# Causal mask of the transposed scores: a GpSimd select on the probabilities in place of one matrix product per diagonal block

## What is computed

```python
qkv = (h @ qkv_w + qkv_b).reshape(B, T, 3, H, HD)
q, k, v = [qkv[:, :, i].transpose(0, 2, 1, 3) for i in range(3)]
attn = jnp.einsum('bhtd,bhsd->bhts', q, k) * scale
causal = jnp.triu(jnp.ones((T, T), bool), 1)
attn = jnp.where(causal[None, None], neg, attn)
attn = jax.nn.softmax(attn, axis=-1)
sa = jnp.einsum('bhts,bhsd->bhtd', attn, v).transpose(0, 2, 1, 3).reshape(B, T, C)
```

## Time and profile before

| what | before |
|---|---|
| median of 3 runs | 2248.85 us (2248.33 to 2249.04) |
| profiled execution | 2250.27 us, its span 2248.3 us |
| TensorE, VectorE, ScalarE, GpSimd busy | 2059.3, 1120.4, 947.7, 774.3 us |
| mean granted TensorE clock | 0.964 |
| attention, from the first unit to the barrier | 116.1 to 381.0 us |
| stacks two to six, first exponential to first exponential | from 150.47, 184.55, 218.63, 252.71 and 286.80 to 320.88: 34.08 or 34.09 us each |
| seventh and eighth stack | from 320.88, from 352.02 to the end |

### The profile page before, as it was taken

One profiled execution on the slowest core, in us unless ns is written; L12 is line 12 of the kernel. 1 busy time (PEld: TensorE's weight loads), 2 busy tenths in 40 slices (PEclk: granted clock), 3 DMA queues, 4 the chain that ended last, 5 costly groups with the idle time before them and its releaser, 6 DMA issues. The chain is left out here.

```text
span 2248.3 us, 27005 instructions
## 1 busy us (share of the span) xinstructions
PE 2059.3 (92%) x10558; PEld 1227.8 (55%) x10558; DVE 1120.4 (50%) x2001; ACT 947.7 (42%) x1443; POOL 774.3 (34%) x511
## 2 busy tenths in 40 slices
PE   5989998798988999999999999999997889899997
PEld 2544444576676754444544454445434867676675
DVE  4666662624445357756455545554542053535353
ACT  4356666233333425555455545554553422222221
POOL 1212100212223126666466646664673011111121
PEclk9999999899998989999999999999999989999999
DMA  7723332000000021000000000000001500000000
GB/s 154 135 31 47 43 54 67 15 1 1 1 1 1 1 64 41 27 1 1 1 1 1 1 1 1 1 1 1 1 1 50 142 7 0 10 1 9 0 10 10
DMA packets 48205, 52.75 MB, mean 23 GB/s; under 512 B 14730, under 2 KB 38988, under 8 KB 47668
## 3 DMA queue, kind: packets, MB, share of 16 engines
q1 hardware_dynamic: 48084, 51.11, 10.9%
HBM read 41.24 MB, written 8.80 MB: 22 GB/s over the span
## 5 line engine op out<-in xcount | busy, mean ns | idle before, releaser
L1825 POOL TENSOR_TENSOR total<-total,pr 128x1024 f32<-128x1024 f32 x192 | 465.3, 2424 | 234.6 <-ACT pr L2021 216.7
L2021 ACT ACTIVATE pr<-sc 128x1024 f32<-128x1024 f32 x256 | 259.8, 1022 | 267.2 <-PE sc L1716 264.6
L1846 DVE TENSOR_REDUCE pmax<-ring 128x1 f32<-128x512 f32 x512 | 314.4, 682 | 98.3 <-PE ring L1664 98.3
L1716 PE MATMUL sc<-q_full,k_full 64*128 64x512 f32 x1024 | 295.0, 589 | 0.0
L1734 PE MATMUL o<-pr,v_pair 128*64 128x512 f32 x1024 | 247.7, 605 | 0.0
L1664 PE MATMUL ring<-k_round,q_round 64*128 64x512 f32 x512 | 213.9, 568 | 6.0 <-DVE k_round L1840 2.0
L629 ACT ACTIVATE probs<-s 128x512 f32<-128x512 f32 (+1 forms) x304 | 163.6, 575 | 106.5 <-PE s L342 59.6
L1029 POOL TENSOR_TENSOR c_scores<-c_scores,c_total 128x1024 f32<-128x1024 f32 (+1 forms) x48 | 77.0, 1614 | 318.9 <-DVE c_total L985 318.9
L463 DVE TENSOR_REDUCE row_max<-s 128x1 f32<-128x640 f32 (+3 forms) x128 | 127.5, 1020 | 52.8 <-PE s L324 52.6
L1664 PEld LDWEIGHTS ring<-k_round,q_round 64*128 64x128 f32 x512 | 78.5, 189 | 137.4 <-DVE pmax L1846 115.3
L1716 PEld LDWEIGHTS sc<-q_full,k_full 64*128 64x128 f32 x1024 | 129.0, 191 | 26.3 <-issue 17.1
(11 more groups left out here) (321 smaller groups left out, 3507.7 us busy)
## 6 DMA issues: line engine op xcount, KB each, us to landing
qk_dram<-qk_parts SPq DMA_DIRECT2D x32, 192.0 KB, 2.7
q_stack<-qk_dram SPq DMA_DIRECT2D x48, 128.0 KB
k_stack<-qk_dram SPq DMA_DIRECT2D x48, 128.0 KB
x<-in_x SPq DMA_DIRECT2D x4, 512.0 KB, 7.7
region<-in_L_xattn_mlp_w SPq DMA_DIRECT2D x2, 1024.0 KB, 7.0
region<-in_L_xattn_ff_w SPq DMA_DIRECT2D x1, 2048.0 KB, 19.2
out<-region SPq DMA_DIRECT2D x8, 256.0 KB, 2.2
region<-in_L_xattn_sa_wo SPq DMA_DIRECT2D x1, 1024.0 KB, 8.1
```

The costliest lines, as they stand in the source:

```text
L1716: ins = te.matmul(s2[at % 2][:, j], kf[n % 2][head[j], keys], qf[n % 2][head[j], halves[half]], start=False, stop=True)
L1825: pool.tensor_tensor(out=total[half][:], in0=other[:], in1=probs[at % KEPT][:], op=ALU.add).then_inc(sums, 1)
L1846: dve.tensor_reduce(part_max[:, j, t, half:half + 1], ring[bank_of_max(i)][:], AX.X, ALU.max).then_inc(s1_free, 1)
L2021: act.activation(probs[here % KEPT][:], s2[at % 2][:], ACT.Exp).then_inc(s2_free, 1)
```

## The change

The mask product in `unit` goes. GpSimd instead sets the entries above the diagonal in `probs` to zero: one `affine_select` of 128 partitions x 4 heads x 128 columns for each of the eight diagonal steps, after the step's last exponential, signalled by the new semaphore `cut`; `values` of these steps waits for it. The splits, clears and bias additions are put between the selects, in one list in the order of the units.

```diff
+        masked_steps = [i for i, (half, kt) in enumerate(VALUES) if start_of(half, kt) == kt * P]
...
+            def cut_step(n, i):
+                pool.wait_ge(exp_made, n * N2 + last_unit[i] + 1)
+                first = probs[(n * N3 + i) % KEPT][:, :, 0:P]
+                pool.affine_select(out=first, in_=first, compare_op=ALU.is_ge, fill=0.0, base=0,
+                                   pattern=[[0, 4], [1, P]], channel_multiplier=-1).then_inc(cut, 1)
+
+
+            split_at = lambda n: min(u for u in range(G * N2) if tops_before(u + 1) >= N1 * (n + 1))
             split(0)
-            for n in range(1, G):
-                split(n)
+            pool.wait_ge(top_split, 4)
+            for n in range(1, G + 1):
+                for step in range(N2):
+                    for i in masked_steps:
+                        if last_unit[i] == step:
+                            cut_step(n - 1, i)
+                    if n < G and split_at(n) == (n - 1) * N2 + step:
+                        pool.wait_ge(cut, len(masked_steps) * (n - 1) + sum(last_unit[i] <= step for i in masked_steps))
+                        split(n)
+                        pool.wait_ge(top_split, 4 * (n + 1))
+                pool.wait_ge(cut, len(masked_steps) * n)
                 if n + 2 < G:
                     clear(n + 2)
+                    pool.wait_ge(rows_cleared, n)
...
-                    pool.wait_ge(rows_cleared, n)
                     x = e.x[:, 4 * n - 4:4 * n, :]
...
-                diagonal = c0 == kt * P
                 for x, j in enumerate(heads):
                     ins = te.matmul(dst[:, x * width:(x + 1) * width], k[:, j, kt * P:(kt + 1) * P],
-                                    q[:, j, c0:c0 + width], start=True, stop=not diagonal)
-                    if diagonal:
-                        ins = te.matmul(dst[:, x * width:x * width + P], tri_bf[:], e.ident_bf[:],
-                                        start=False, stop=True)
+                                    q[:, j, c0:c0 + width], start=True, stop=True)
                 ins.then_inc(s2_made, 1)
...
                 te.wait_ge(exp_made, n * N2 + last_unit[i] + 1)
+                if i in masked_steps:
+                    te.wait_ge(cut, len(masked_steps) * n + masked_steps.index(i) + 1)
```

More of the change, by code:

```diff
@@ L122, in part_attention0 @@
             sem(n) for n in ("s1_made", "s1_free", "top_split", "top_out", "top_in"))
+        cut = sem("cut")
         s2_made, exp_made, pv_made, raw_made, turned, inverted, sa_made = (
```

## The result

The changed kernel takes 2254.27 us (median of 19 runs, 2251.82 to 2257.82) against 2251.12 for the kernel before (19 runs in the same job, 2248.33 to 2253.97). The ratio is 1.0015, interval 1.0008 to 1.0022: 3.4 us slower, 1.8 to 5.0. The forecast was 2.3 us faster. The runs of each kernel are spread over 5.6 and 6.0 us now, which the first three runs of the kernel before had not shown.

What follows compares the result with a forecast made beforehand. TensorE was taken to set the pace, 31.81 of 34.08 us busy in a middle stack. Savings of 9.45 us against stalls and the tail summed to -2.3 us, from 2248.85 to 2246.5 us, range 2241.5 to 2259.

Steps and rivals of the forecast that it cites:

- The price of a select: On GpSimd, one select of 128x4x128 takes 0.61 us, between 0.30 from below and 1.15 from above.
- The path from exponential to product: From a step's last exponential to its values product: signal 0.07, select 0.61, signal 0.06, together 0.74 us.
- The change of stacks: Ahead of kt 0's values product, selects, clear and add chain to 7.47 us: 1.49 late at four changes, 5.96 in all.
- the other changes of stack: Changes of stack without the bias addition: no stall, and removed mask products save 0.35 us together.
- The middle of a stack: Between first values product and last exponential: 25 mask products save 1.38 us a stack, about 0.08 lost at kt 4, no stall.
- The tail: Attention's end, without row maxima: select waits cost 2.0 us, removed mask products give 1.0, net 1.0 us slower.
- The sum: Whole kernel: -9.45 + 0.5 - 0.35 + 5.96 + 1.0 = -2.3 us, so faster.
- if the mask products win less than 1.3 us a stack: One of three signs named in advance that would show the forecast wrong; it concerns the saving in each stack.
- rival 2: At the four changes of stack the clock falls, losing 3.4 us each time: 2260.1 us; chance 0.04.
- The range: Whole kernel's time: 2241.5 to 2259 us, with no more than a tenth beyond each end.
- within 0.2%: Whole kernel: the forecast case, a select between 0.45 and 0.87 us, giving 2243.5 to 2252 us; chance 0.60.
- The dearer select: Rival 1, on GpSimd: a select of 0.93 us gives 2255.1, of 1.15 gives 2261.9, so slower; chance 0.22.

Runs made afterwards that it cites:

- no_mask: The kernel before without the mask product of the transposed scores and without a select; ratio to before 0.9959, a middle stack 33.01 us.
- both: The changed kernel with the removed mask products put back, so selects and products together; ratio to the kernel before 1.0036.

## Why the prediction was wrong, point by point

- **The price of a select**, 0.61 us, held (0.637). So did the choice between the two estimates worked out from the Trainium skill (GPSIMD Engine Reference, Performance pitfalls for Q7 kernels), 0.94 and 0.62 us: the trace agrees with the second. The path from exponential to product is 0.82 us against 0.74, where the product waits for the select in the tail. At kt 1 the slack left is 0.82 as well (in `no_mask`, where no select runs; forecast 0.83), so the select just fits there, with nothing of the tenth to spare.
- **The change of stacks** held: chain 7.6 for 7.47, idle where forecast, four times (1.87 us, not 1.5). The cost is 1.49 us with the products kept (`both`) and 1.6 without them, as forecast within 0.1 each: 0.4 us of error. That the other changes of stack save 0.35 did not hold, they save nothing.
- **The middle of a stack** is the first term that was mis-sized, and the step that failed. "25 x 0.055 = 1.38" less 0.08, that is 1.30, was to be saved in each stack; it was 1.00 (34.08 to 33.08 us). No select stalled there. Product by product, the traces before and after of the sixth stack, from its first values product to that of the next stack, show where TensorE lost the rest. All 32 removed products (25 and the 7 ahead of the next kt 0) are worth 1.76 us at 0.055, and up to kt 4 they give that to within 0.02. By kt 7 0.16 is lost, nearly all of it about kt 4, where I had 0.08. At kt 7 another 0.44 goes at the wait for VectorE. Ahead of the next kt 0 0.16 of the last seven products' 0.39 goes in the chain of copy, transposition and gather, where I had counted on none of the 0.39. 1.76 - 0.16 - 0.44 - 0.16 = 1.00. So I looked for waits on ScalarE and on the select alone, and took VectorE, 23.5 of 34 us busy, as having room: at kt 7 eight short products (four score, four mask) had covered its reduction, and the four that are left do not. `no_mask` shows the 0.33 us wait with no select in the program. Six stacks: 1.7 us.
- **The tail** was to be 1.0 us slower, with 0.5 saved ahead of it in stack 7: net 0.5. It is 0.96. `no_mask` prices the products at 2.0 us there (I had 1.5) and the selects at 3.0 (I had 2.0).
- **The sum** with these terms corrected is -2.3 + 0.4 + 0.35 + 1.7 + 0.5 = +0.7 us, already on the other side of zero. The forecast was a difference of two terms of 9 and 7 us, and errors of 3.0 us in all, most of them in what the removed products give, turned its sign. The prediction had named the sign of this: "if the mask products win less than 1.3 us a stack".
- **The clock**, rival 2, I had given 0.04. A stall of 1.7 to 1.9 us brought it down in 7 of 14 cases, at 1.4 to 1.6 us and not at 3.4. Four stalls at one in two are an estimate of 3.2 us, and 0.7 + 3.2 = 3.9 agrees with the 3.4 (1.8 to 5.0) measured. The step that failed was reading two isolated stretches as if an idle either does it or does not. The profiled execution had one fall: 0.7 + 1.6 = 2.3, and its attention is 2.4 us longer. That in the timed runs the falls are as frequent as in the profiles is not shown. Their mean granted clock points that way: 0.9620 over the 19 runs of the changed kernel, 0.9630 over 38 runs of the kernel before in the next two jobs. That is an estimate of 4.7 us more at half clock, about 1.4 falls of 3.4 us with an uncertainty of one, and it doesn't say in which stage.
- **The range** of the time held it, and the case "within 0.2%" was the right one, with the other sign; 2254.27 lies above that case's own 2243.5 to 2252. The dearer select, the rival that I gave most, did not occur.

## What to carry to other kernels

Before a piece of work moves to an idle engine, write down what stands ahead of it in that engine's list: here a clear and an addition that no product had waited for became a stall of 1.9 us that cost 1.6, and moving them behind unit 10 of the next stack turned a loss of 0.15% into a gain of 0.2%. When short instructions are taken from the pacing engine, ask for each wait behind them whose work they had covered, on every engine that frees a buffer. And where a wait is made, count the clock with it: a rate over several profiles says more than one stretch.

## What the runs showed of the hardware

An idle of 1.86 to 1.88 us on TensorE amid dense work was followed by 3.4 us at 1.2 GHz in six of ten cases, one of 1.67 us (`both`) in one of four, one of 5.41 us by 6.8 us at 1.2 GHz in all four, and one of 3.0 us, once, by none. Nor did the clock fall at the idles of 1.10 us, one a stack in each of the first seven stacks before the change. An affine select of 128 partitions x 4 x 128 in fp32 took 0.637 us, 1.23 for two back to back, where one of 128x128 had taken 0.294.
